# Query rotation through PSUM, stores of the query groups by ScalarE, a context ring of nine tiles, and a later reciprocal product in the even steps

## The reference

```python
# x: 8 x 56 x 512, context: 8 x 1500 x 512, 32 query heads in 8 groups of 4, head size 128
q = rope((layernorm(x) @ wq) per head)          # 8 x 32 x 56 x 128
k = rope((context @ wk) per group)              # 8 x 8 x 1500 x 128
v = (context @ wv) per group
attn = softmax(q @ k.T / sqrt(128) + mask) @ v
x = x + tanh(g_xattn) * (attn @ wo)
x = x + tanh(g_ffn) * lora_experts(layernorm(x))  # 4 experts, top 2, rank 16
# rope(t) = t * cos + rotate_half(t) * sin
```

## Time and profile before

| | us |
|---|---|
| median of 3 runs (2132.41 to 2134.17) | 2133.44 |
| the profiled execution | 2150.03 |
| its span on the core | 2148.3 |
| TensorE (PE) busy | 2021.8 (94%) |
| VectorE (DVE) busy | 1279.3 (60%) |
| ScalarE (ACT) busy | 1047.5 (49%) |
| GpSimd (POOL) busy | 312.1 (15%) |

### The profile page before, as it was taken

How to read it: one execution, slowest core, us unless ns; L and a number is a source line. 1 busy time by engine, 2 the same in 40 slices (tenths; PEclk the granted TensorE clock), 3 DMA queues, 4 the chain that set the end, 5 groups by cost and what they waited for, 6 DMA issues and landing times. The chain is left out here.

```text
span 2148.3 us, 36505 instructions
## 1 busy us (share of the span) xinstructions
PE 2021.8 (94%) x12372; PEld 1791.7 (83%) x12372; DVE 1279.3 (60%) x2639; ACT 1047.5 (49%) x1756; POOL 312.1 (15%) x221
## 2 busy tenths in 40 slices
PE   7779999999989999899989998899999999999898
PEld 6668887889978998799978998788888998999676
DVE  7965666556655666556655666566655666666534
ACT  4444555445554555445554445455544554555522
POOL 4511111111111111111111110111111111111200
PEclk9989999999999999999999999999999999999898
DMA  5441111101121112111121112101211112111260
GB/s 189 149 154 43 14 14 51 37 14 14 14 54 42 14 14 51 43 12 14 16 53 38 14 14 55 39 14 14 40 44 23 14 14 53 33 14 14 76 223 26
DMA packets 74962, 95.00 MB, mean 44 GB/s; under 512 B 22692, under 2 KB 49444, under 8 KB 74760
## 3 DMA queue, kind: packets, MB, share of 16 engines
q1 hardware_dynamic: 74760, 92.44, 18.6%
HBM read 76.64 MB, written 15.77 MB: 43 GB/s over the span
## 5 line engine op out<-in xcount | busy, mean ns | idle before, releaser
L624 POOL TENSOR_TENSOR k_lo<-k_work,k_hi 128x500 fp32r<-128x500 f32 x192 | 244.4, 1286 | 1648.5 <-ACT k_hi L656 1648.5
L753 PE MATMUL sv_banks<-wv_hi,cT_hi 128*125 128x256 f32 x1536 | 443.7, 289 | 0.0
L753 PE MATMUL sv_banks<-wv_hi,cT_lo 128*125 128x256 f32 x1536 | 431.5, 281 | 0.0
L753 PE MATMUL sv_banks<-wv_lo,cT_hi 128*125 128x256 f32 x1536 | 431.4, 281 | 0.0
L949 DVE TENSOR_TENSOR pT<-t_banks,pT 125x448 fp32r<-125x448 f32 x384 | 236.3, 623 | 262.9 <-ACT pT L717 262.9
L717 ACT ACTIVATE pT<-t_banks 125x448 fp32r<-125x448 f32 x384 | 205.2, 543 | 346.0 <-PE t_banks L789 345.1
L924 DVE CUSTOM_DVE_ANT_0 prob<-sv_banks,mask_t 112x500 f32<-112x500 f32 x384 | 258.5, 678 | 187.3 <-PE sv_banks L777 181.4
L737 PE MATMUL k_banks<-cT_hi,wk_hi 128*128 128x500 f32 x768 | 318.7, 415 | 35.5 <-DVE k_work L862 25.7
L695 ACT ACTIVATE prob<-prob,neg_max 112x1500 f32<-112x1500 f32 x128 | 198.6, 1552 | 276.9 <-DVE neg_max L929 276.1
L737 PE MATMUL k_banks<-cT_hi,wk_lo 128*128 128x500 f32 x768 | 303.3, 395 | 0.0
L737 PE MATMUL k_banks<-cT_lo,wk_hi 128*128 128x500 f32 x768 | 303.3, 395 | 0.0
(11 more groups left out here) (125 smaller groups left out, 2987.0 us busy)
## 6 DMA issues: line engine op xcount, KB each, us to landing
stage<-in_ctx_dram SPq DMA_DIRECT2D x96, 250.0 KB
attn_by_head<-attn SPq DMA_DIRECT2D x65, 112.0 KB, 1.7
wq_raw<-in_L_xattn_wq_dram SPq DMA_DIRECT2D x7, 1024.0 KB, 6.3
q_raw<-q_by_head SPq DMA_DIRECT2D x64, 112.0 KB, 4.4
inv_b<-inv_by_head SPq DMA_DIRECT2D x64, 112.0 KB, 4.7
mask_t<-in_mask_BxSxS_ff_dram SPq DMA_DIRECT2D x16, 328.1 KB
stage<-in_L_xattn_wo_dram SPq DMA_DIRECT2D x4, 1024.0 KB, 5.5
k_work<-in_L_xattn_wo_dram SPq DMA_DIRECT2D x4, 1024.0 KB, 6.3
```

The lines of the kernel that those rows point to most:

```text
L624: nc.gpsimd.tensor_tensor(k[1][:, c * SC:(c + 1) * SC], k_rot[:, s], f32(k[0][:, c * SC:(c + 1) * SC]), ALU.subtract).then_inc(k_lo, 1)
L753: mm = nc.tensor.matmul(sv_banks[0:ST, m % 2, t * PAIR:(t + 1) * PAIR], cT[a][:, d, tile * ST:(tile + 1) * ST], w[1][mv][:, d, g * DH:g * ...
```

## The change

In the query part the exchanged halves go to the PSUM banks of `xT_banks` (free once x has been transposed and split; four of them, one for each head of a group). VectorE multiplies these with the sine into a new SBUF buffer `q_sine`, multiplies the q bank with the cosine in place in PSUM, and adds the two into `q_rot[u]`; the q bank is free only after the addition, the exchange bank after the sine product. ScalarE makes the high part of wk or wv ahead of the four exchanges instead of between them, and issues the store of a group itself, behind the second exchange of the group after it (the last one at the end).

In the attention part the ring has nine slots, six in `stage` and three in `head_rows`. At the start the three tiles for `head_rows` are loaded once the last query group has been stored from it. In step 0 nine tiles of the next batch are loaded, and in the turn step only tiles 9 to 11. In the even steps `norm` stands behind `rot1` instead of behind `max1`.

```diff
-STAGE_RING = NT // 2
+STAGE_TILES = NT // 2
+HEAD_TILES = REP * TOK // D
+STAGE_RING = STAGE_TILES + HEAD_TILES
...
-    "even": ("mask0 mask1 mask2 mask3 max0 mask4 mask5 max1 norm cos0 sin0 rot0 cos1 T0 T1 sin1 rot1 T2 Q V4 inv cos2 T3 "
+    "even": ("mask0 mask1 mask2 mask3 max0 mask4 mask5 max1 cos0 sin0 rot0 cos1 T0 T1 sin1 rot1 norm T2 Q V4 inv cos2 T3 "
...
+        head_tiles = self.head_rows[:, :, :, :].rearrange("p b h s -> p (b h s)")[:, 0:HEAD_TILES * D].rearrange("p (t d) -> p t d", d=D)
+        self.c_slots = [(self.stage if n < STAGE_TILES else head_tiles)[0:ST, n % STAGE_TILES, :] for n in range(STAGE_RING)]
...
-                wait_apart(sp, q_rotated, i * heads2 + (u + 1) * REP, sp_passed)
-                dst = q_dram[bass.ds(i * 2 + u, 1)].rearrange("g p b n -> p (g b n)")
-                sp.dma_start(dst, q_rot[u][:, :, :, :].rearrange("p b h s -> p (b h s)")).then_inc(q_stored[u], 16)
...
+                act.wait_ge(shared.w_loaded[u], i * 16 + 16)
+                nc.scalar.activation(w[u][0][:, bass.ds(i, 1), :], shared.w_stage[u][:, None, :],
+                                     ACT.Copy).then_inc(w_hi, 1)
                 for hh in range(REP):
 
                     act.wait_ge(q_ready, i * heads2 + (u * REP + hh + 1))
 
-                    act.wait_ge(swap_free, i * heads2 + (u * REP + hh + 1))
+                    act.wait_ge(q_sined, i * heads2 + (u * REP + hh + 1))
                     for lo in range(2):
-                        nc.scalar.activation(
-                            q_swap[lo * HALF:(lo + 1) * HALF, hh % 2].rearrange("p b s -> p (b s)"),
-                            q_banks[(1 - lo) * HALF:(2 - lo) * HALF, hh, 0:TOK], ACT.Copy).then_inc(q_swapped, 1)
...
+                        nc.scalar.activation(xT_banks[lo * HALF:(lo + 1) * HALF, hh, 0:TOK],
+                                             q_banks[(1 - lo) * HALF:(2 - lo) * HALF, hh, 0:TOK], ACT.Copy).then_inc(q_swapped, 1)
+                    if hh == 1 and not (first and u == 0):
+                        store_group(i * 2 + (u - 1), 1 - u)
+
+        def store_group(n, u):
+
+            act.wait_ge(q_rotated, (n + 1) * REP)
+            act.dma_start(q_dram[bass.ds(n, 1)].rearrange("g p b n -> p (g b n)"),
+                          q_rot[u][:, :, :, :].rearrange("p b h s -> p (b h s)")).then_inc(q_stored[u], 16)
...
-                    nc.vector.tensor_tensor(q_part[:, s], q_banks[:, hh, 0:TOK].rearrange("p (b s) -> p b s", b=B),
-                                            cos_b, ALU.mult).then_inc(q_free, 1)
-                    nc.vector.tensor_tensor(q_swap[:, s], q_swap[:, s], sin_b, ALU.mult).then_inc(q_sined, 1)
...
+                    nc.vector.tensor_tensor(q_sine[:, s], xT_banks[:, hh, 0:TOK].rearrange("p (b s) -> p b s", b=B),
+                                            sin_b, ALU.mult).then_inc(q_sined, 1)
+                    nc.vector.tensor_tensor(bank, bank, cos_b, ALU.mult).then_inc(q_cosined, 1)
+                    dve.wait_ge(q_sined, i * heads2 + (REP + n + 1))
+                    dve.wait_ge(q_cosined, i * heads2 + (n + 1))
+                    nc.vector.tensor_tensor(q_rot[u][:, :, hh, :], bank, q_sine[:, s], ALU.add).then_inc(q_rotated, 1)
                     dve.wait_ge(q_rotated, i * heads2 + (n + 1))
-                    dve.sem_inc(swap_free, 1)
+                    dve.sem_inc(q_free, 1)
...
         sp.wait_ge(shared.q_stored[1], 16 * (HKV // 2 + 1))
+        for m in range(STAGE_TILES, STAGE_RING):
+            load_context(nc, sp, shared, ctx_v, 0, m)
         load_q(0, 1)
         for m in range(STAGE_RING, NT):
```

More of the change, by code:

```diff
@@ L174, in __init__ @@
         self.w = [[sb(f"{n}_{h}", [P, DC, HKV * DH], F32R) for h in ("hi", "lo")] for n in ("wk", "wv")]
-        self.stage = sb("stage", [P, STAGE_RING, D])
-        self.w_stage = [self.stage[:, n * (STAGE_RING // 2):n * (STAGE_RING // 2) + 2, :].rearrange("p t d -> p (t d)") for n in range(2)]
+        self.stage = sb("stage", [P, STAGE_TILES, D])
+        self.w_stage = [self.stage[:, n * (STAGE_TILES // 2):n * (STAGE_TILES // 2) + 2, :].rearrange("p t d -> p (t d)") for n in range(2)]
         self.tables = sb("k_tables", [P, 2, SK])
@@ L214, in load_context @@
     slot = m % STAGE_RING
-    sp.dma_start(shared.stage[0:ST, slot, :], ctx_v[bass.ds(b, 1), m].rearrange("b p d -> p (b d)")).then_inc(shared.stage_loaded[slot], 16)
+    sp.dma_start(shared.c_slots[slot], ctx_v[bass.ds(b, 1), m].rearrange("b p d -> p (b d)")).then_inc(shared.stage_loaded[slot], 16)
 def load_mask(sp, shared, mask, b):
@@ L274, in query_part @@
     wq_hi, wq_lo = sem("wq_hi_ready"), sem("wq_lo_ready")
-    q_ready, q_free, q_swapped, q_sined, q_rotated = (
-        sem(n) for n in ("q_ready", "q_free", "q_swapped", "q_sined", "q_rotated"))
-    swap_free = sem("q_swap_free")
+    q_ready, q_free, q_swapped, q_sined, q_cosined, q_rotated = (
+        sem(n) for n in ("q_ready", "q_free", "q_swapped", "q_sined", "q_cosined", "q_rotated"))
     x_v = x.rearrange("(t b) s d -> (b s) t d", t=NTT)
@@ L320, in two_groups @@
                 else:
-                    for m in range(u * (STAGE_RING // 2), (u + 1) * (STAGE_RING // 2)):
+                    for m in range(u * (STAGE_TILES // 2), (u + 1) * (STAGE_TILES // 2)):
                         load_context(nc, sp, shared, context_views(ctx_in), 0, m)
-                wait_apart(sp, q_rotated, i * heads2 + (u + 1) * REP, sp_passed)
-                dst = q_dram[bass.ds(i * 2 + u, 1)].rearrange("g p b n -> p (g b n)")
-                sp.dma_start(dst, q_rot[u][:, :, :, :].rearrange("p b h s -> p (b h s)")).then_inc(q_stored[u], 16)
         sp.wait_ge(first_lo, REP)
@@ L384, in _, with two_groups @@
             nc.scalar.activation(xT[0][:, c, :], xT_banks[:, c, 0:TOK], ACT.Copy).then_inc(xT_hi, 1)
-        def two_groups(i, last):
+        def two_groups(i, first, last):
             for u in range(2):
@@ L390, in two_groups @@
                     split_wq(i * 2 + (u + 1), 1 - u)
+                act.wait_ge(shared.w_loaded[u], i * 16 + 16)
+                nc.scalar.activation(w[u][0][:, bass.ds(i, 1), :], shared.w_stage[u][:, None, :],
+                                     ACT.Copy).then_inc(w_hi, 1)
                 for hh in range(REP):
                     act.wait_ge(q_ready, i * heads2 + (u * REP + hh + 1))
-                    act.wait_ge(swap_free, i * heads2 + (u * REP + hh + 1))
+                    act.wait_ge(q_sined, i * heads2 + (u * REP + hh + 1))
                     for lo in range(2):
-                        nc.scalar.activation(
-                            q_swap[lo * HALF:(lo + 1) * HALF, hh % 2].rearrange("p b s -> p (b s)"),
-                            q_banks[(1 - lo) * HALF:(2 - lo) * HALF, hh, 0:TOK], ACT.Copy).then_inc(q_swapped, 1)
[L400 to L408, removed]
+                        nc.scalar.activation(xT_banks[lo * HALF:(lo + 1) * HALF, hh, 0:TOK],
[6 more added lines that the diff above has]
+                          q_rot[u][:, :, :, :].rearrange("p b h s -> p (b h s)")).then_inc(q_stored[u], 16)
+        two_groups(0, True, False)
+        with act.Fori(1, pairs - 1) as i:
+            two_groups(i, False, False)
+        two_groups(pairs - 1, False, True)
+        store_group(HKV - 1, 1)
     @block.tensor
@@ L446, in _ @@
         dve.sem_inc(q_free, REP)
-        dve.sem_inc(swap_free, 2)
+        dve.sem_inc(q_sined, REP)
         for t in range(NTT):
@@ L542, in c_stage_ready @@
     def c_stage_ready(eng, b, m):
-        eng.wait_ge(stage_loaded[m % STAGE_RING], b * 32 + 16 * (m // STAGE_RING + 1))
+        slot = m % STAGE_RING
+        loads = len(range(slot, NT, STAGE_RING))
+        eng.wait_ge(stage_loaded[slot], b * (16 * loads) + 16 * (m // STAGE_RING + 1))
     def c_tile(m):
-        return stage[0:ST, m % STAGE_RING, :]
+        return shared.c_slots[m % STAGE_RING]
     block = ctx.enter_context(nc.Block())
```

10 lines of the change are left out of this document (3 added, 7 removed).

## The result

The changed kernel takes **2115.64 us** (median of 4 runs, 2112.97 to 2117.36) against 2132.93 before (4 runs, 2131.28 to 2134.17): ratio 0.9915, 95% interval 0.9901 to 0.9929, 17.3 us faster. The forecast was 2111.4, 4.2 us too low, with a range of 2094 to 2126.

A forecast was written before the change was run, and what follows sets the result against it. The prediction took TensorE, busy 94% of the span, as the bound, with VectorE setting the query part's end. Its terms summed to -22.0 us: 2128.0 from the profiled 2150.03, 2111.4 off the median 2133.44, range 2094 to 2126.

The forecast's parts named there:

- Query part, -30.2: Query part: VectorE's stalls beside GpSimd go, TensorE becomes the bound, the last addition ends at 97.3 instead of 127.5 us.
- The unknown cost of writing PSUM: Query part: VectorE's and ScalarE's PSUM writes taken to cost no more than SBUF; doubled, the gain is 24 or 12 us.
- Start of the attention part, -3.0: Attention start: -1.5 us from less half clock after TensorE's shorter pause, -1.5 from tiles 6 to 11 starting earlier.
- Turn steps, -35.7: Seven turn steps: waits for context tiles go, 5.1 us each, total between -26 and -45.
- Nine tiles in step 0, +42.7: Seven batches: three more tiles queued ahead of the reciprocals delay `norm` and TensorE in step 1 by 6.1 us each.
- clock, +4.2: Step 1, seven batches: TensorE's longer stand costs 0.6 us more at half clock each, total 0 to +8.
- `norm` in the even steps, 0: Even steps: moving `norm` behind `rot1` costs nothing; 13 us over 32 steps if the cover went.
- The rival that the reciprocals are not held up further: Step 0: three more tiles only fill a DMA gap, +42.7 and +4.2 vanish, 2064.5 us; chance 1 in 10.
- that of a query part bound by ScalarE or the wq loads: Query part: bound at 11 to 12 us a group, gaining 12 to 24 us, 2123.6 with 18; chance 16 in 100.
- the slower one: Query part: VectorE still stops for GpSimd wherever inputs lie, no gain there, +8.2 us, 2141.6; chance 6 in 100.

The follow-up runs named there:

- Experiment 2: The kernel before with only the changed query part (exchange into PSUM, stores by ScalarE, early copy of wk or wv): 2115.33 us, ratio 0.9861 to before.
- 6: The kernel before with only the exchange and the cosine product moved to PSUM: 2117.72 us, ratio 0.9879 to before.
- experiment 7: The kernel before with only ScalarE's stores and the early copy of wk or wv, exchange still in SBUF: 2142.17 us, ratio 0.9990 to before.
- second pair: Profiles of the unedited kernel before and of the changed kernel, each run again, on two other chips: their spans differ by 21.6 us.
- Experiment 8: The changed kernel with the nine tile loads of step 0 issued behind the load of the reciprocals: 2038.56 us, ratio 0.9503 to before.
- 11: The changed kernel with tile loads behind the reciprocals of step 0 and a ring of six tiles instead of nine: 2082.62 us, ratio 0.9695 to before.
- 4: The changed kernel with `norm` of the even steps back in its old place: 2123.17 us, ratio 0.9898 to before.
- experiment 5: The changed kernel once more, unedited, on another chip: 2124.34 us, ratio 0.9903 to before.
- experiment 12: The changed kernel with the nine tile loads behind the reciprocals of step 0 and each tile loaded as 112 and 13 rows: 2038.37 us, ratio 0.9496 to before.
- experiment 9: The changed kernel with the store and load of the reciprocals of step 0 issued by ScalarE on its own queue: 2078.10 us, ratio 0.9667 to before.

## Why the prediction was right, and where it was off

The mechanisms were those of the forecast, and what it named as their signs came: `inv_b` 25.2 us after the first tile (25.4 forecast), `norm` waiting 9.68 us (10.5), TensorE 60.2 and 64.7 us in all (70), its first context transposition at 99.45 (98.6). Its steps, by the two pairs of profiles:

- **Query part, -30.2:** -29.1, from 127.5 to 98.36 us. Experiment 2 gives 29.8 by its ratio, 6 and 7 that it is the stalls. The unknown cost of writing PSUM was nothing: VectorE's L487 takes 0.62 us, ScalarE's 64-partition copy 517 ns (540 into SBUF in experiment 7). The missing 1.1 us is the first exchange, at 19.06 instead of 17.83 us, since ScalarE's early copy of wk stands ahead of it (1.07 us): a cost of the order of ScalarE's work that the sum left out.
- **Start of the attention part, -3.0:** about -1.4; from the last addition to T0 of batch 0 it is 44.0 us instead of 45.4. The step that failed is the clock. TensorE's pause did shrink to 4.11 us, but it then worked at half clock from 99.45 to about 105.7 and lost the same 3.1 us. Half clock after a pause didn't shrink with the pause, so of this term only the half for the earlier tiles came.
- **Turn steps, -35.7:** 7 x -5.2 = -36.5, and 7 x -5.3 in the second pair. Experiments 8 and 11 give 41.
- **Nine tiles in step 0, +42.7, and clock, +4.2:** the stretches T0 to C0 grew by 7 x 5.1 = +36.0 in the first pair and 7 x 6.9 = +48.4 in the second, on either side of the 46.9 forecast. TensorE's wait grew by 34.5 and 42.6 us. Its loss to half clock in the first 8 us after the stands was 16.7 us in the profile of after against 12.3, +4.4, and 14.3 against 9.1 in the second pair. Experiment 8 shows the cause and its whole price: both the part that before already paid and the part that the change added. The forecast put the added 6.1 us a batch into the queue ahead of the reciprocals; the rows show them in SyncE's issuing ahead of their store, and the same size.
- **`norm` in the even steps, 0:** experiments 4 and 5.

By the sum it is -22.0; by the ratio of experiment 5, 0.9903, -20.7; on the chip of the result -17.3. The 4 us between forecast and result there were not located. Before is 13 us faster there than on the chip of experiment 5, after only 9. If the stand in step 1 more often costs before no clock there, as in three of seven batches of the second profile of before, that would do it; no profile shows it. In the first pair, whose profile of before the forecast was built on, the terms above make -31.0 of the -32.7 us, 9 more than the sum, and step 0 alone is 10.9 off; in the second they make about -20 of the -21.6. So the total came within 5 us, while the term of step 0 spreads by 12 us between pairs, and the close total is in part luck.

The rival that the reciprocals are not held up further fell with the 9.08 us; that of a query part bound by ScalarE or the wq loads fell too, TensorE having no wait in it; and the slower one with the undisturbed L487. The upper bound of 2126 was said to take in the second of these in whole; with its smallest gain of 12 us it reaches 2129.6. The query part came out far from it, so nothing hung on that.

## What to carry to other kernels

A large prefetch that is in no hurry belongs behind the small transfers that someone waits for, in the program order of its queue: here the kernel is 86 us slower with the nine loads ahead of 900 bytes of reciprocals than with them behind, where loads of twice the rate (experiment 12) bring nothing more. Moving one small transfer to another queue helps only that one: in experiment 9 the next load in the old queue took up the delay. A change that moves time little can hold two large terms of opposite sign; price each by itself, and look where the added work queues before giving up on it. A stand of TensorE costs more than its length: ask for the clock behind it as well.

## What the runs showed of the hardware

- VectorE with both inputs in SBUF stopped for GpSimd's SBUF work (up to 4.9 us for an instruction of 0.62); with one input in PSUM it didn't, whether it wrote PSUM or SBUF (0.62 us each).
- DMAs of 125 rows moved at 128 GB/s with a third of the engines busy; in pieces of 112 and 13 rows at 252 GB/s.
- SyncE issued the first six of nine such tiles in 3.6 us and took 6.2 us for the last three.
- A transfer of 0.9 KB on ScalarE's queue passed tiles queued by SyncE, 9.3 us to landing against about 13; a load of 112 KB right behind the tiles in SyncE's queue took 13 to 18 us instead of 4.3.
- TensorE's stands ahead of a key product, in the 14 profiles of this case, and what it lost to half clock in the 8 us behind them: after 8.2 to 9.7 us 1.4 to 3.0 us, in 28 of 28; after 2.75 to 4.15 us up to 2.9 us in 26 of 35, and nothing in 9; after 1.0 to 2.0 us nothing in 84 of 93, and 1.7 us in 9.
